# One-hot tiles built by eighteen column compares in place of one block-wide compare

## The reference, cut to what matters

```python
W = jnp.einsum('rb,bde->rde', comp, basis)
h = jnp.einsum('nd,rde->nre', x, W)
msg = h[src, edge_type]
seg = dst * R + edge_type
sums = jax.ops.segment_sum(msg, seg, num_segments=n * R)
cnt = jax.ops.segment_sum(jnp.ones((msg.shape[0],), msg.dtype), seg, num_segments=n * R)
mean = sums / jnp.maximum(cnt, 1.0)[:, None]
agg = mean.reshape(n, R, -1).sum(axis=1)
return agg + x @ root + bias
```

## Time and profile before

| | busy us | share of the span | instructions |
|---|---|---|---|
| PE | 3842.3 | 79% | 38119 |
| DVE | 3017.5 | 62% | 6579 |
| ACT | 881.8 | 18% | 2470 |
| POOL | 3331.7 | 69% | 3374 |

### The profile page before, as it was taken

How to read it: one execution, slowest core, us unless ns; L and a number is a source line. 1 busy time by engine, 2 the same in 40 slices (tenths; PEclk the granted TensorE clock), 3 DMA queues, 4 the chain that set the end, 5 groups by cost and what they waited for, 6 DMA issues and landing times.

```text
span 4838.2 us, 119647 instructions
## 1 busy us (share of the span) xinstructions
PE 3842.3 (79%) x38119; PEld 3300.8 (68%) x38120; DVE 3017.5 (62%) x6579; ACT 881.8 (18%) x2470; POOL 3331.7 (69%) x3374
## 2 busy tenths in 40 slices
PE   1366666666666666666469999999999999999999
PEld 1255555555555555555358888888888888888888
DVE  4556656666666566666456666666666666666663
ACT  1200000000000000000013333333333333333333
POOL 0477777777777777777477676767676777676770
PEclk6555555555555555555569999999999999999999
DMA  4656655555555555555465555555555555555551
GB/s 129 192 171 183 176 158 156 157 158 158 155 157 159 156 157 158 158 156 157 117 169 166 156 159 155 158 154 158 154 158 156 158 157 160 154 160 154 159 158 22
DMA packets 344661, 749.10 MB, mean 155 GB/s; under 512 B 128323, under 2 KB 167806, under 8 KB 344430
## 3 DMA queue, kind: packets, MB, share of 16 engines
q0 software_dynamic: 215040, 662.09, 48.7%
q1 hardware_dynamic: 115510, 70.49, 5.6%
q10 hardware_dynamic: 14076, 16.04, 1.0%
HBM read 719.00 MB, written 29.35 MB: 155 GB/s over the span
## 4 chain that ended last, share of the span: by engine, by line
PE 59%; issue 12%; DVE 12%; POOL 9%; DMA 8%; DVEq 0%; SPq 0%; ACT 0%; POOLq 0%; ACTq 0%
PE bank L1351 15%; PE bank L1338 14%; PE bank L1251 11%; POOL slot L558 9%; PE bank L1283 8%; DMA slot<-table,idx 6%; DVE inv L939 4%; PE bank L1247 3%; DVE scaled L945 3%; PE bank L1311 3%; PE bank L1312 2%; DVE mixed L913 2%; PE bank L1279 1%; DVE inv L938 1%; PE bank L1314 1%
## 5 line engine op out<-in xcount | busy, mean ns | idle before, releaser
L558 POOL DMA_INDIRECT slot<-table,idx x3354 | 3326.0, 992 | 1342.0 <-issue 1085.2
L1251 PE MATMUL bank<-hot,slot 128*128 (+1 forms) x21168 | 1380.1, 212 | 67.5 <-DMA slot<-table,idx 60.6
L1251 PEld LDWEIGHTS bank<-hot,slot 128*128 128x128 bf16 x21168 | 1112.1, 108 | 219.4 <-issue 75.0
L1247 PE MATMUL bank<-hot,ones_b 128*128 x1764 | 398.7, 226 | 745.4 <-DMA slot<-table,idx 340.1
L1338 PE MATMUL bank<-xnT,ffn_w 128*128 128x128 f32 x6272 | 867.1, 285 | 20.0 <-DVE scaled L945 20.0
L1247 PEld LDWEIGHTS bank<-hot,ones_b 128*128 128x128 bf16 x1764 | 181.0, 103 | 1006.4 <-issue 969.2
L1351 PE MATMUL bank<-ffn_w,act 128*128 128x256 f32 x3136 | 842.0, 395 | 0.3 <-DVE o L1024 0.3
L1338 PEld LDWEIGHTS bank<-xnT,ffn_w 128*128 128x128 f32 x6272 | 755.8, 192 | 46.4 <-DVE scaled L945 28.8
L1351 PEld LDWEIGHTS bank<-ffn_w,act 128*128 128x128 f32 x3136 | 541.1, 191 | 60.7 <-issue 16.9
L913 DVE SCALAR_TENSOR_TENSOR mixed<-scaled,small,mixed 128x256 f32<-128x256 f32 x1372 | 573.7, 480 | 12.2
L913 DVE SCALAR_TENSOR_TENSOR mixed<-scaled,comp_sb,mixed 128x256 f32<-128x256 f32 x1372 | 573.5, 480 | 10.5
(11 more groups left out here) (148 smaller groups left out, 2192.0 us busy)
## 6 DMA issues: line engine op xcount, KB each, us to landing
slot<-table,idx POOLq DMA_INDIRECT x3354, 3.1
inv<-inv_d SPq DMA_DIRECT2D x98, 256.0 KB, 3.8
table<-ffn_w SPq DMA_DIRECT2D x7, 1344.0 KB, 6.0
table<-parts ACTq DMA_DIRECT2D x49, 192.0 KB, 3.1
ffn_w<-in_L_ffn_W_dram SPq DMA_DIRECT2D x16, 512.0 KB
xcur<-in_x_dram SPq DMA_DIRECT2D x48, 128.0 KB
out_dram<-o ACTq DMA_DIRECT2D x48, 128.0 KB
ffn_w<-in_x_dram SPq DMA_DIRECT2D x6, 896.0 KB, 9.0
```

What stands on the lines that cost most here:

```text
L558: gp.indirect_dma_start(out=slot[:, k, :], out_offset=None, in_=table[layer], in_offset=bass.IndirectOffsetOnAxis(ap=idx[:, h, k:k + 1], a ...
L1247: t.matmul(C[:, at], ones_b[:, :], oh, start=(k == 0), stop=(k == TILES - 1), skip_group_check=True)
L1251: last = t.matmul(S[f][:, at], slot[:, k, q * D + f * P:q * D + (f + 1) * P], oh, start=(k == 0 and q == 0), stop=(k == TILES - 1 and q == ...
```

## The change

The single compare with two broadcast operands is replaced by 18 compares of `iota_b` with a scalar column of `rel`, each of which writes one tile. The last one signals.

```diff
@@ -926,9 +926,9 @@
             def one_hots_fast(h, G):
                 dve.wait_ge(idx_in[h], G * 48 + 48)
                 summed(dve, G, h, back=2)
-                v.tensor_tensor(hot[:, h, :, :], iota_b[:, :].unsqueeze(1).broadcast_to([P, TILES, COLS]),
-                                rel[:, h, :].unsqueeze(2).broadcast_to([P, TILES, COLS]),
-                                ALU.is_equal).then_inc(hot_ready, 1)
+                for k in range(TILES):
+                    last = v.tensor_scalar(hot[:, h, k, :], iota_b[:, :], rel[:, h, k:k + 1], None, ALU.is_equal)
+                last.then_inc(hot_ready, 1)
```

## The result

The changed kernel takes 4847.7 us (median of 16 runs, 4838.5 to 4872.1) against 4837.35 us before (16 runs, 4835.3 to 4839.7): a ratio of 1.0027, 95% interval 1.0017 to 1.0037 (ratios here and below are taken over all runs of both kernels, so they can differ a little from the quotient of the medians). It is slower by 10 us. I had forecast 4867 us, +30: the sign is right, the size three times too large. Not forecast at all was the spread of the runs, 34 us in place of 4.

What follows compares the result with a forecast made beforehand. Layer 0 was taken as bound by POOL's gathers, layer 1 by PE with L945 behind the h=1 compare. 4840.0 + 79 - 48, about 1 back, gave 4870, or 4867 us for the median; range 4812 to 4940.

Steps and rivals of the forecast that it cites:

- the 0.3 us a pair: Layer 0: allowance for gathers slowed beside the new compares, with bounds 0 and 1.29 us.
- the compares' price: DVE: 18 compares at 0.16 us a step take 3.0 us in place of 1.35, 1.65 us more a block.
- the count of bodies in layer 1: Layer 1: 48 bodies that load a further pair each pay 1.65 us, +79 us.
- the clock: Rival, chance 0.05: PE's longer stalls in layer 1 lower its granted clock, 2.5 us lost each time, 120 us, 4987 us.
- What bounds each layer: Layer 0: POOL's gathers, held 1.29 us a pair by the old compare; layer 1: PE, waiting for L945 behind h=1's compare.
- X: DVE time for the series of 18 compares: 3.0 us taken, between 2.45 and 4.95; break-even at 2.35.
- Layer 1: the cost: L945 and PE's next block come 1.65 us later in 48 bodies, +79 us; compares for h=0 cost nothing.
- Layer 0: the gain: Held gathers go, less an allowance: POOL's pair falls from 44.06 to 43.07 us, 0.99 us a pair, -48 us.
- The loop through DVE and PE: Layer 0: 39.7 us plus the series, 42.7 us a pair, just under POOL's 43.07; DVE bounds from a 3.4 us series.
- The near balance: Rival, chance 0.12: step 0.12 to 0.14 us and free gathers, or layer 1's cost hidden: within 10 us, 4837.
- Gathers held for the whole series: Rival, chance 0.05: layer 0's holds each grow by 1.65 us, +158 us in place of -48, 5073 us.
- Cheap and dear compares: Two rivals, chance 0.14 each: step 0.10 us, -33 us, 4804 us; or step about 0.21 us, +100 us, 4937 us.

Runs made afterwards that it cites:

- experiment 1: The kernel before with the 18 compares in one layer only: layer 0 only 4774.5 us, layer 1 only 4903.3 us, against 4837.9 before.
- experiment 2: Changed kernel, in layer 1: block-wide compare back for h=1, 4775.4 us; or 12 more compares ahead of the series for h=0, 4914.8 us.
- experiment 6: Changed kernel with, in layer 1 for h=1, 6 compares ahead of L945 and the other 12 behind it, with their own signal: 4768.4 us.
- experiment 4: Changed kernel with PE multiplying ones (12 products) ahead of its wait in layer 1: 4838.4 us, ratio 1.0003 to the kernel before.

## Why the prediction was right or wrong

The mechanism and the sign were right, the size was not: +30 us forecast, +10 measured. What failed is the sizing of the sum's terms, in three places: the 0.3 us a pair that layer 0 was charged for gathers beside the short compares (measured: about 0), the compares' price and the count of bodies in layer 1 (+79 forecast, +61 measured without dips), and the clock, which the sum put at nothing (measured: some 19 us). The parts below take them one by one.

*What bounds each layer.* Right. Layer 0 was POOL's, held gathers included: POOL's gathers there are 63.1 us shorter and the layer 65.1. Layer 1 was L945 behind the compare for h=1. Experiments 1, 2 and 6 show both.

*The price of the compares.* Forecast X = 3.0 us at a step of 0.16. Measured 2.75 to 2.78 us in layer 1, (2.77 - 0.24) / 17 = 0.149 us a step, and 3.02 us for the series beside `mix_bases` in layer 0. The row that I took for nearest (one scalar column, step 0.13) was the right one; what I added for the columns at L911's rate, 0.03, was too much: 0.02 was enough. The prediction's other estimate, with the four elements a cycle of the Trainium skill (VectorE: DVE Perf Modes, The perf-mode tier table), was a step of 0.15 and X about 2.8, and this trace agrees with it.

*Layer 1: the cost.* The mechanism is as forecast, the term too large: a pair grew by 1.36 us and not 1.65, most of it because X is 2.77 and not 3.0. And it is paid 46 times and not 48: the first two bodies have no expert yet, and no such stall shows in them. 46 x 1.36 = 63 and not 79. In experiment 4, where no dip is left, the rest of the span is 61.1 us longer.

*Layer 0: the gain.* The step that failed here is the allowance of 0.3 us a pair for gathers still held: it was about 0. I had taken it from gathers beside L913, 1.01 in place of 0.95 us, but those were in the 44.06 us of before already; beside the new compares a gather takes 0.95 and 0.96. A pair fell by some 1.3 us in place of 0.99, and the gain is 65 us, not 48. The loop through DVE and PE was put at 39.7 + X = 42.7 (its terms add up to 39.6). A pair takes 42.8, but that is no test of it, as POOL alone gives the same: 44.06 - 1.29 = 42.77. POOL never pauses for more than 0.31 us between gathers in the pair shown, while the chain that ended last runs there over DVE's mixing and compares. So the two are about level, and more compares should cost in layer 0 too; no run tested this.

*The clock.* The rival had a chance of 0.05 and 120 us, for a dip that costs 2.5 us in every pair. It does occur, in 12 of 46 pairs at 1.6 us, some 19 us in the profiled execution, and the sum had no term for it. The reasoning against it, that 2.1 of 48 us is a small gap, was wrong: a gap of 1.8 us was enough in a quarter of the pairs. It is also why the runs spread.

*The sum.* -65 for layer 0, +61 for layer 1 without dips, +18 for the dips: +14, as in this execution. The first two were forecast 17 and 18 us too high and the third, left out, gives 18 back, so two errors of the sum cancelled by luck and the forecast missed by 17 us and not by 35. The median of the runs is at +10, which fits a few dips less.

*The other rivals.* The near balance (step 0.12 to 0.14, free gathers, within 10 us of no change) comes nearest in number: the gathers were free, the step of 0.149 lies just above it, and with the dips filled in experiment 4 the kernel is 1.7 us from before. Its other reading, a cost that stays hidden in layer 1, is excluded by experiment 1. Gathers held for the whole series: excluded, the longest gather takes 1.22 us. What the Trainium skill says of two-port instructions (Advanced Engine Details and Errata, VectorE Performance Modes) did not show itself beside the short compares, where gathers take 0.95 and 0.96 us. Cheap and dear compares: excluded by the step.

## What to carry to other kernels

Where a small effect is the difference of two large ones, make the edit only where it pays: the same one was worth -63 us where POOL was the bound and +65 where DVE stood in front of PE, and a series of small instructions can be laid around an urgent one (experiment 6). Where PE runs at 2.4 GHz, a longer wait can cost more than it adds: 1.37 us more of stall made a pair with a dip 3.0 us longer. A spread between runs is a sign to look for, but only of dips that come now and then: the kernels with dips in 46 and 38 of 46 pairs had two and four runs that lay within 2 us of each other.

## What the runs showed of the hardware

- A VectorE compare with two broadcast tensors in SBUF holds an indirect DMA of GpSimd that starts beside it: the DMA ends 0.82 us behind the compare's end, so 0.95 us becomes 1.83 in the pair shown and up to 2.15 in the trace. With three such compares in a row a gather is held to the end of the first (1.04 us), the second or the last (1.50, up to 2.29); what decides is open. 18 short compares with a scalar column don't hold one (0.96 us), nor do chained `scalar_tensor_tensor` of 256 columns (1.01). What separates the chained ones from the compares that hold is open.
- TensorE's clock fell to 1.2 GHz behind stalls of 1.8 us in 12 and 7 of 46 pairs, behind 1.92 us in 46, behind 3.11 us in 38, and behind 1.22 us or less in none. With 3.11 us some dips last longer and cost 2.7 us in place of 1.6. Dips often come in neighbouring pairs; whether a pair that is lengthened by one brings on the next, or the stall's length does it, is open.
- In three of seven sittings PE starved inside its stream, for 0.5 to 1.1 us at a time in the rows shown, and there none of the gains above survived: even the kernel that won 69 us was 32 us slower than before.
